# Sixteen-head cross-attentions: four row groups of TensorE share the score matmuls, and each context's column scores go four heads at a time

## The chip, the cores and the metric

One core of one Trainium2 chip runs the whole program. The metric is the device time of one execution in microseconds (us), as the median of several runs. The kernel before takes 1945.53 us (median of 3 runs, 1936.75 to 1956.92).

## The reference, cut to what matters

A model of four layers; each has a cross-attention block and a feed-forward block, on x of 4 sequences x 512 tokens x 128 features, with a context of 4 x 77 x 64. The change touches three of the attentions: layer 0's (`l0x`, 16 heads of 8 features), the second one of layer 1 (`a2`, 16 heads of 32 features) and layer 3's (`l3x`, 16 heads of 8). All three are the same computation:

```python
qh = (q @ Wq + bq).reshape(B, LQ, HEADS, D_K).transpose(0, 2, 1, 3)      # 512 queries, 16 heads
kh = (k @ Wk + bk).reshape(B, LKV, HEADS, D_K).transpose(0, 2, 1, 3)     # 77 keys
vh = (v @ Wv + bv).reshape(B, LKV, HEADS, D_K).transpose(0, 2, 1, 3)
scores = jnp.einsum('bhqd,bhkd->bhqk', qh, kh) * scale
attn = jax.nn.softmax(scores, axis=-1)
out = jnp.einsum('bhqk,bhkd->bhqd', attn, vh)
...
return concat @ Wo + bo
```

Everything else (the layer norms, layer 1's causal attentions, the routed experts of layers 1 to 3) is computed too and is not changed.

## The kernel before, in words

Features lie on the 128 partitions, tokens along the free dimension. The sequences are worked on two at a time (`U = range(SLOTS)`, u = 0 and 1); a hardware loop makes two turns (`Fori(0, TURNS)`), and each turn runs `l0x`, `a2` and `l3x` once. So there are six passes through `cross(tag, dh)`: four with dh = 8 and two with dh = 32. Each engine has its own `cross` (TensorE from line 618, ScalarE from 1562, VectorE from 1920); they meet at counted semaphores only. The order of the work on each engine is written out by hand.

A pass does this:

- **Row scores R(u, a)**, a = 0 to 7, `rowscores` (matmuls on lines 641 for dh = 8 and 645 for dh = 32): queries on the partitions, for two values of c, four heads' 77 keys each. With dh = 8 a matmul uses one row group (c = 2 hf + b, hf = a % 2); with dh = 32 it uses all 128 rows, so nothing can run beside it. VectorE takes their maxima (`maxima`, line 1927).
- **cut off and turned**: the maxima are split in two bf16 halves (`cut_off`) and transposed (`turned`, line 654), and ScalarE copies them out (`shifted`, line 1565).
- **Column scores T(u, a)**, a = 0 to 7, `colscores` (line 670): keys on the partitions, 512 queries, for two heads (k = a // 2, c = 2 hf + b). Two float32 matmuls of 32 x 512, then two bf16 ones that subtract the maxima in the same PSUM bank. I call these last **less**, after the variable. ScalarE takes the exponentials of both heads (`exp`, line 1574).
- **sums** (line 681, dh = 32 alone) and **values** (line 695): four matmuls side by side in four column groups over all 77 keys, for the four heads of one k. They use all the rows.

The two sequences overlap: R(0, .) come first, alone. In what I call **phase 1** TensorE does T(0, a), R(1, a) for a = 0 to 7, with values(0, k) behind a = 3, 5, 7 and once more at the end, and then turned(1). In **phase 2** it does T(1, a), with values(1, k) behind a = 3, 5, 7. A **pair** below is the stretch of two values of a, with the sums and values that belong to it.

R and T share three slots of two PSUM banks each, in turn: `cplace` gives the place of each step in that ring, `cbefore` tells what was three places before, and `free(x)` makes TensorE wait until VectorE's maximum or ScalarE's exponential has read it. In phase 1 T(0, a) has place 9 + 2a and R(1, a) place 10 + 2a. So R(1, a) waits for the exponential of T(0, a - 1), and T(0, a) for the maximum of R(1, a - 2). In phase 2 T(1, a) waits for the exponential of T(1, a - 3). `values(u, k)` waits for the exponential of T(u, 2k + 1) with dh = 8; with dh = 32 it waits for ScalarE's copy `o` (line 1586) of the values before, which ScalarE does behind two later exponentials.

## Time and profile before

| | |
|---|---|
| median of 3 runs | 1945.53 us (1936.75 to 1956.92) |
| profiled execution, whole | 1932.59 us |
| its span, first to last instruction | 1930.5 us |
| mean granted TensorE clock in it | 0.87 of full |
| instructions | 22528 |

### The profile page before, as it was taken

What the parts mean: (1) busy time and instruction counts of PE and PEld (TensorE: products, weight loads), DVE (VectorE), ACT (ScalarE), POOL (GpSimd) and SP (SyncE); (2) the same over time, 40 slices, a digit from 0 to 9 for tenths busy, and PEclk for the clock granted to TensorE, in tenths of its full rate; (3) what the DMA queues carried; (4) which work ended last, traced back from release to release, by engine and by line L of the source; (5) the groups of instructions that cost most, each with busy time, mean ns of one, the idle gap of its engine ahead of it and who ended that gap; (6) DMA issues with size and microseconds to landing.
All of it is one profiled execution on the core that took longest, in us unless ns stands there. A gap on an engine that the chain in (4) does not pass through costs nothing.

```text
span 1930.5 us, 22528 instructions
## 1 busy us (share of the span) xinstructions
PE 1643.6 (85%) x9068; PEld 762.3 (39%) x9068; DVE 880.0 (46%) x1746; ACT 715.9 (37%) x1267; POOL 146.9 (8%) x207
## 2 busy tenths in 40 slices
PE   5748999989899989997648999989899989988487
PEld 2323333332344536633323323332343436543274
DVE  4474664253456353324474663353456352337312
ACT  2333455324435225232332455323445125243133
POOL 0000011100012000000000111100012000002232
PEclk9768899989989699956768999989999689889688
DMA  4000000000000100000000000000000100002241
GB/s 178 1 1 0 1 2 1 1 1 1 0 1 1 44 1 1 1 1 2 1 1 0 1 1 1 0 1 1 0 1 2 44 1 1 1 33 44 62 135 59
DMA packets 18107, 30.17 MB, mean 16 GB/s; under 512 B 4640, under 2 KB 12640, under 8 KB 17104
## 3 DMA queue, kind: packets, MB, share of 16 engines
q1 hardware_dynamic: 16752, 26.10, 4.2%
q0 software_dynamic: 1248, 2.59, 0.4%
q8 instruction: 74, 1.21, 0.3%
q14 instruction: 33, 0.27, 0.0%
HBM read 23.49 MB, written 5.19 MB: 15 GB/s over the span
## 4 chain that ended last, share of the span: by engine, by line
PE 78%; DVE 12%; ACT 7%; issue 2%; DMA 1%; SPq 0%; POOL 0%; POOLq 0%; DVEq 0%; ACTq 0%
PE ps L783 8%; PE ps L881 5%; PE ps L670 5%; PE ps L613 3%; PE ps L815 3%; PE ps L1323 3%; PE ps L1335 3%; PE ps L1020 3%; PE ps L695 3%; PE ps L1012 3%; PE ps L932 2%; PE ps L829 2%; PE ps L1242 2%; PE ps L912 2%; PE ps L804 2%
## 5 line engine op out<-in xcount | busy, mean ns | idle before, releaser
L2000 DVE TENSOR_REDUCE peak<-ps 128x1 f32<-128x512 f32 x256 | 165.4, 686 | 119.0 <-PE ps L783 118.4
L1620 ACT ACTIVATE big<-ps 128x512 f32<-128x512 f32 x256 | 139.6, 595 | 133.8 <-PE ps L806 126.9
L783 PE MATMUL ps<-pp,qT 32*128 32x512 f32 x512 | 169.5, 714 | 3.5 <-DVE peak L2000 2.1
L804 PE MATMUL ps<-qT,pp 32*128 32x512 f32 x512 | 160.4, 649 | 0.0
L1641 ACT ACTIVATE big<-ps 128x512 f32<-128x512 f32 (+3 forms) x256 | 100.3, 436 | 112.5 <-PE ps L912 111.7
L2037 DVE TENSOR_REDUCE crest<-ps 128x2 f32<-128x512 f32 (+3 forms) x128 | 105.2, 825 | 65.7 <-PE ps L887 65.6
L1574 ACT ACTIVATE big<-ps 77x1024 f32<-77x1024 f32 x96 | 94.7, 1019 | 95.8 <-PE ps L670 95.2
L912 PE MATMUL ps<-qT,pp 32*128 32x256 f32 (+3 forms) x512 | 124.4, 494 | 0.9 <-ACT big L1641 0.9
L1927 DVE TENSOR_REDUCE small<-ps 128x8 f32<-128x616 f32 x96 | 74.2, 797 | 102.8 <-PE ps L641 58.1
L881 PE MATMUL ps<-pp,qT 32*128 32x384 f32 (+3 forms) x512 | 109.2, 501 | 9.5 <-DVE crest L2037 8.5
L1555 ACT ACTIVATE sq<-ps 128x512 f32<-128x512 f32 x52 | 31.1, 597 | 204.4 <-PE ps L613 204.4
L670 PE MATMUL ps<-qT,kt 32*77 32x512 f32 x384 | 94.1, 741 | 9.8 <-ACT spare L1565 9.6
L783 PEld LDWEIGHTS ps<-pp,qT 32*128 32x128 f32 x512 | 59.2, 202 | 83.4 <-DVE peak L2000 65.9
L542 POOL TENSOR_SCALAR_AFFINE_SELECT big<-big 128x512 f32<-128x512 f32 x64 | 40.8, 637 | 616.4 <-PE ps L815 616.4
L560 POOL TENSOR_SCALAR_AFFINE_SELECT big<-big 128x512 f32<-128x512 f32 x64 | 40.8, 637 | 555.9 <-ACT big L1641 555.9
L1879 DVE TENSOR_TENSOR xn<-ps,rs 128x512 f32<-128x512 f32 x40 | 27.7, 692 | 94.0 <-ACT rs L1560 94.0
L815 PE MATMUL ps<-big,cst 128*32 128x512 f32 x512 | 68.1, 604 | 0.0
L1012 PE MATMUL ps<-xn,w_l 128*128 128x512 f32 x96 | 51.7, 699 | 18.1 <-DVE xn L1884 18.1
L1778 ACT ACTIVATE big<-ps,w_l 128x512 f32<-128x512 f32 x64 | 44.0, 687 | 59.1 <-PE ps L1323 57.5
L695 PE MATMUL ps<-big,vx 77*32 77x512 f32 x384 | 58.3, 690 | 6.0 <-ACT qT L1586 6.0
L1335 PEld LDWEIGHTS ps<-pt,big 128*128 128x128 f32 x512 | 59.4, 192 | 6.7 <-issue 6.7
L806 PE MATMUL ps<-spare,minus 32*128 32x512 bf16 x256 | 61.4, 377 | 0.0
(484 smaller groups left out, 2775.3 us busy)
## 6 DMA issues: line engine op xcount, KB each, us to landing
big<-in_w SPq DMA_DIRECT2D x23, 256.0 KB
pt<-in_l2w SPq DMA_DIRECT2D x2, 2048.0 KB, 7.5
w_l<-in_l SPq DMA_DIRECT2D x1, 3086.0 KB, 17.3
pp<-in_w SPq DMA_DIRECT2D x1, 2048.0 KB, 9.6
big<-by_expert SPq DMA_DIRECT2D x23, 66.0 KB, 2.0
by_expert<-cst SPq DMA_DIRECT2D x1, 1472.0 KB, 16.3
cst<-in_const SPq DMA_DIRECT2D x1, 1298.0 KB, 5.8
w_l<-in_l SPq DMA_DIRECT2D x1, 1218.0 KB, 8.0
```

The source lines that it names most:

```text
L670: mm = pe.matmul(PSB[cbank(x) + b][0:KC, :], keys, query, start=not less, stop=less, tile_position=(32 * c, 0))
L695: mm = pe.matmul(PSB[k // 2 if dh == 8 else 0][32 * c:32 * c + 32, :], vx[:, u, at:at + 32], cprob(u, k)[:, c, :], start=dh == 32 or k % 2 ...
L783: pe.matmul(rbank(x), qT[at, u, k, 128 * i:128 * i + 128], keyT(u, k)[at, :], start=True, stop=True, tile_position=(32 * c, 0)).then_inc(* ...
L804: pe.matmul(tbank(y), keyT(u, k)[at, 128 * j:128 * j + 128], qT[at, u, k, :], start=True, stop=False, tile_position=(32 * c, 0))
L815: mm = pe.matmul(PSB[1][32 * c:32 * c + 32, :], K["col8"][:, 128 * k + 32 * c:128 * k + 32 * c + 32], prob(n)[:, c, :], start=n % 16 == 0, ...
L881: pe.matmul(PSB[pbank(x) + c % 2][:, 0:hi], qT[at, u, k, 128 * i:128 * i + 128], keyT(u, k)[at, 0:hi], start=True, stop=False, tile_positi ...
L912: pe.matmul(tbank(y)[:, lo:512], keyT(u, k)[at, 128 * j:128 * j + 128], qT[at, u, k, lo:512], start=True, stop=True, tile_position=(32 * c ...
L1012: pe.matmul(scb(c), w[:, 128 * c:128 * c + 128], src(u), start=True, stop=True)\
L1335: mm = pe.matmul(lin(u)[:, 128 * i:128 * i + 128], hid[u][:, c, 128 * i:128 * i + 128], W2[:, 128 * c:128 * c + 128], start=c == 0, stop=c ...
L1620: A(prob(m)[:, TURN_OF[g], :], tbank(tplace(m, g)), ACT.Exp).then_inc(*SCALAR.did("a1", "exp", m, g))
L2000: v.tensor_reduce(peak[:, p // 4 % 2, i, c:c + 1], rbank(ring(p, c)), AX.X, ALU.max)\
L2037: v.tensor_reduce(crest[:, u, i, 2 * h:2 * h + 2, k], ps[:, b:b + 2, 0:hi], AX.X, ALU.max)\
```

## The change

In the order of the diff:

- The ring's places change. With dh = 8 phase 1 keeps the places (T(0, a) at 9 + 2a, R(1, a) at 10 + 2a). With dh = 32 they go in fours: T(2k), T(2k + 1), R(2k), R(2k + 1). So T(0, 2k) waits for the exponential of T(0, 2k - 1), and R(1, 2k + 1) for that of T(0, 2k).
- With dh = 8 the half of the row groups that R(1, a) uses is turned round (`half_of`): it takes the two that T(0, a) leaves.
- `colscores(u, a)` becomes single steps `colscore(u, a, b, less)`. `colscores4(u, k)` issues the float32 matmuls of four heads and then their four less; it replaces two `colscores` in all of phase 2, and in phase 1 with dh = 32. The new `colscores(a)`, for phase 1 with dh = 8, issues R(1, a) ahead of T(0, a)'s less where a is odd, and behind it where a is even.
- In phase 1 with dh = 8 values(0, k - 1) moves from behind R(1, 2k + 1) to between R(1, 2k) and T(0, 2k + 1). With dh = 32 sums and values stand behind each group of T, T, R, R, as before in count. The last values(0, 3) stays ahead of turned(1).
- The number of matmuls, their shapes, the reductions, the exponentials and the copies stay as they are.

```diff
--- before.py
+++ after.py
@@ -301,16 +301,18 @@
 
         TURN_OF = (2, 3, 0, 1)
 
-        def cplace(kind, u, a=0):
-
-
-            if kind == "R":
-                return a if u == 0 else 10 + 2 * a
+        def cplace(dh, kind, u, a=0):
+
+
+
             if kind == "turned":
                 return 8 if u == 0 else 25
-            return 9 + 2 * a if u == 0 else 26 + a
-
-        def cbefore(x):
+            if (kind == "R") == (u == 0):
+                return a if u == 0 else 26 + a
+            later = kind == "R"
+            return 9 + 2 * a + later if dh == 8 else 9 + 4 * (a // 2) + a % 2 + 2 * later
+
+        def cbefore(dh, x):
 
             z = x - 3
             if z < 0:
@@ -319,9 +321,16 @@
                 return "R", 0, z
             if z == 8 or z == 25:
                 return "turned", z // 25, 0
-            if z < 25:
-                return ("T", 0, (z - 9) // 2) if z % 2 else ("R", 1, (z - 10) // 2)
-            return "T", 1, z - 26
+            if z > 25:
+                return "T", 1, z - 26
+            z -= 9
+            if dh == 8:
+                return ("R", 1, z // 2) if z % 2 else ("T", 0, z // 2)
+            return ("R", 1, 2 * (z // 4) + z % 2) if z % 4 >= 2 else ("T", 0, 2 * (z // 4) + z % 2)
+
+        def half_of(dh, u, a):
+
+            return (a + u) % 2 if dh == 8 else a % 2
 
         def cbank(x):
             return 2 + 2 * (x % 3)
@@ -619,7 +628,7 @@
 
 
                 def free(x):
-                    h = cbefore(x)
+                    h = cbefore(dh, x)
                     if h and h[0] == "R":
                         pe.wait_ge(*VECTOR[tag, "max", h[1], h[2]])
                     elif h and h[0] == "turned":
@@ -628,8 +637,8 @@
                         pe.wait_ge(*SCALAR[tag, "exp", h[1], h[2]])
 
                 def rowscores(u, a):
-                    i, hf = a // 2, a % 2
-                    x = cplace("R", u, a)
+                    i, hf = a // 2, half_of(dh, u, a)
+                    x = cplace(dh, "R", u, a)
                     free(x)
                     if a == 0:
                         pe.wait_ge(*VECTOR[tag, "kv", u])
@@ -647,7 +656,7 @@
                     mm.then_inc(*TENSOR.did(tag, "R", u, a))
 
                 def turned(u):
-                    x = cplace("turned", u)
+                    x = cplace(dh, "turned", u)
                     pe.wait_ge(*VECTOR[tag, "cut", u])
                     free(x)
                     for i in range(4):
@@ -655,21 +664,38 @@
                                           cut[:, i].rearrange("p c r -> p (c r)"), identb[:])
                     mm.then_inc(*TENSOR.did(tag, "turned", u))
 
-                def colscores(u, a):
-                    k, hf = a // 2, a % 2
-                    x = cplace("T", u, a)
-                    free(x)
-                    if a == 0:
-                        pe.wait_ge(*SCALAR[tag, "shift", u])
+                def colscore(u, a, b, less):
+                    k, c = a // 2, 2 * (a % 2) + b
+                    x = cplace(dh, "T", u, a)
+                    if not less and b == 0:
+                        free(x)
+                        if a == 0:
+                            pe.wait_ge(*SCALAR[tag, "shift", u])
+                    at = slice(32 * c, 32 * c + 32)
+                    keys = minus[at, k:k + 1].to_broadcast([32, KC]) if less else kt[at, u, k, :]
+                    query = shift[at, u, :] if less else qT[at, u, 0 if dh == 8 else k, :]
+                    mm = pe.matmul(PSB[cbank(x) + b][0:KC, :], keys, query, start=not less, stop=less,
+                                   tile_position=(32 * c, 0))
+                    if less and b:
+                        mm.then_inc(*TENSOR.did(tag, "T", u, a))
+
+                def colscores4(u, k):
+
                     for less in (False, True):
-                        for b in (0, 1):
-                            c = 2 * hf + b
-                            at = slice(32 * c, 32 * c + 32)
-                            keys = minus[at, k:k + 1].to_broadcast([32, KC]) if less else kt[at, u, k, :]
-                            query = shift[at, u, :] if less else qT[at, u, 0 if dh == 8 else k, :]
-                            mm = pe.matmul(PSB[cbank(x) + b][0:KC, :], keys, query, start=not less, stop=less,
-                                           tile_position=(32 * c, 0))
-                    mm.then_inc(*TENSOR.did(tag, "T", u, a))
+                        for a in (2 * k, 2 * k + 1):
+                            for b in (0, 1):
+                                colscore(u, a, b, less)
+
+                def colscores(a):
+
+                    colscore(0, a, 0, False)
+                    colscore(0, a, 1, False)
+                    if a % 2:
+                        rowscores(1, a)
+                    colscore(0, a, 0, True)
+                    colscore(0, a, 1, True)
+                    if a % 2 == 0:
+                        rowscores(1, a)
 
                 def sums(u, k):
                     if dh == 8:
@@ -725,20 +751,27 @@
                 for a in range(8):
                     rowscores(0, a)
                 turned(0)
-                for a in range(8):
-                    colscores(0, a)
-                    rowscores(1, a)
-                    if a >= 3 and a % 2:
-                        sums(0, (a - 3) // 2)
-                        values(0, (a - 3) // 2)
+                for k in range(4):
+                    if dh == 8:
+                        colscores(2 * k)
+                        if k:
+                            values(0, k - 1)
+                        colscores(2 * k + 1)
+                    else:
+                        colscores4(0, k)
+                        rowscores(1, 2 * k)
+                        rowscores(1, 2 * k + 1)
+                        if k:
+                            sums(0, k - 1)
+                            values(0, k - 1)
                 sums(0, 3)
                 values(0, 3)
                 turned(1)
-                for a in range(8):
-                    colscores(1, a)
-                    if a >= 3 and a % 2:
-                        sums(1, (a - 3) // 2)
-                        values(1, (a - 3) // 2)
+                for k in range(4):
+                    colscores4(1, k)
+                    if k:
+                        sums(1, k - 1)
+                        values(1, k - 1)
                 if dh == 8:
                     heads(0, 0)
                     heads(0, 1)
@@ -1562,12 +1595,12 @@
             def cross(tag, dh):
                 def shifted(u):
                     act.wait_ge(*TENSOR[tag, "turned", u])
-                    A(shift[:, u, :], PSB[cbank(cplace("turned", u))].bitcast(BF16)[:, 0:512], ACT.Identity)\
+                    A(shift[:, u, :], PSB[cbank(cplace(dh, "turned", u))].bitcast(BF16)[:, 0:512], ACT.Identity)\
                         .then_inc(*SCALAR.did(tag, "shift", u))
 
                 def exp(u, a):
                     k, hf = a // 2, a % 2
-                    b = cbank(cplace("T", u, a))
+                    b = cbank(cplace(dh, "T", u, a))
                     act.wait_ge(*TENSOR[tag, "T", u, a])
                     if u and hf == 0:
                         act.wait_ge(*TENSOR[tag, "AV", 0, k])
@@ -1919,8 +1952,8 @@
 
             def cross(tag, dh, bv=None):
                 def maxima(u, a):
-                    i, hf = a // 2, a % 2
-                    b = cbank(cplace("R", u, a))
+                    i, hf = a // 2, half_of(dh, u, a)
+                    b = cbank(cplace(dh, "R", u, a))
                     v.wait_ge(*TENSOR[tag, "R", u, a])
                     top = tops(u)[:, i, 2 * hf:2 * hf + 2, :] if dh == 8 else \
                         tops(u)[:, i, :, 2 * hf:2 * hf + 2].rearrange("p c k -> p k c")
```

## Rows read from the trace of the kernel before

**Rows 1.** the page: span, busy time by engine, the chain by engine

```profile
span 1930.5 us, 22528 instructions
...
PE 1643.6 (85%) x9068; PEld 762.3 (39%) x9068; DVE 880.0 (46%) x1746; ACT 715.9 (37%) x1267; POOL 146.9 (8%) x207
...
PE 78%; DVE 12%; ACT 7%; issue 2%; DMA 1%; SPq 0%; POOL 0%; POOLq 0%; DVEq 0%; ACTq 0%
```

**Rows 2.** windows, phase 1: length, busy of PE PEld DVE ACT POOL, clock

```profile
1687.65:1705.27 17.62, 16.05 (x112) 5.88 (x113) 7.23 (x11) 8.32 (x9) 0.00 (x0) 0.91 0.00 1
428.51:455.58 27.07, 27.07 (x144) 9.78 (x145) 6.85 (x10) 9.73 (x11) 0.00 (x0) 1.00 0.00 1
```

**Rows 3.** windows of the four whole passes of l0x and l3x

```profile
41.97:72.84 30.87, 28.66 (x205) 11.63 (x205) 7.98 (x12) 17.61 (x20) 0.00 (x0) 0.89 0.00 1
824.21:867.09 42.88, 41.73 (x205) 14.56 (x205) 7.98 (x12) 17.93 (x20) 0.00 (x0) 0.57 0.00 1
905.43:939.18 33.75, 31.91 (x204) 12.44 (x204) 7.98 (x12) 17.67 (x20) 0.00 (x0) 0.79 0.00 1
1687.65:1717.66 30.01, 27.57 (x204) 10.74 (x204) 7.98 (x12) 17.50 (x20) 0.00 (x0) 0.95 0.00 1
```

**Rows 4.** the chain of waits, 440 to 448 us (a2): start, us, what

```profile
440.30 1.23 PE ps L670 x6
441.53 1.23 PE ps L645 x4
...
445.23 1.00 PE ps L681 x8
446.23 0.86 PE ps L695 x8
```

**Rows 5.** the chain of waits, 51 to 56 us (l0x)

```profile
51.33 1.25 PE ps L670 x8
...
52.60 1.03 ACT big L1574
...
53.68 0.79 PE ps L641 x4
54.46 1.00 PE ps L695 x8
```

**Rows 6.** timeline of l0x, 51 to 53 us: start, us, engine, line, records

```profile
51.26 1.16 PE L670 MATMUL ps<-qT,kt 32*77 32x512 f32 x6
...
52.18 0.38 PE L670 MATMUL ps<-spare,minus 32*77 32x512 bf16 x2
...
52.26 0.59 PE L670 MATMUL ps<-qT,kt 32*77 32x512 f32 x2
...
52.40 0.68 PE L641 MATMUL ps<-kt,qT 32*128 32x308 f32 x4
```

**Rows 7.** timeline of l0x, end of phase 1 and a stretch of phase 2

```profile
58.58 1.92 PE L695 MATMUL ps<-big,vx 77*32 77x512 f32 x16
...
60.44 0.40 PE L654 MATMUL ps<-identb,spare 128*128 128x128 bf16 x4
...
66.32 1.16 PE L670 MATMUL ps<-qT,kt 32*77 32x512 f32 x8
```

**Rows 8.** the chain of waits, 462 to 472 us (a2, phase 2)

```profile
466.32 1.06 PE ps L695 x8
467.38 1.25 PE ps L670 x12
...
468.65 1.93 ACT big L1574 x2
470.58 0.49 ACT qT L1586
```

**Rows 9.** windows of TensorE alone around a fall of its clock (l0x)

```profile
39.00:42.00 3.00, 0.43 (x6) 1.00 0.00 0
42.00:45.00 3.00, 3.00 (x16) 0.55 0.00 0
```

## The prediction

> **What bounds the kernel now.** The page first: TensorE is busy for 85% of the span and holds 78% of the chain that ended last [rows 1]. That share says nothing about one stage, so the next view is the windows: phase 1 of a pass takes 27.07 us in `a2` at full clock with PE busy for all of it, and 17.62 us in the best of the four dh = 8 passes, at a granted clock of 0.91 [rows 2]. The four whole dh = 8 passes take 30.87, 42.88, 33.75 and 30.01 us, in the order of their clocks, 0.89, 0.57, 0.79 and 0.95 [rows 3]: the same instructions, so a low clock costs more here than most edits could give.
>
> The chain of waits of `a2` shows a pair in phase 1 as pure TensorE work: T 1.23, R 1.23, twice each, then sums 1.00 and values 0.86 [rows 4], 4 x 1.23 + 1.86 = 6.78 us. Four times 4.92 and four times 1.86 make 27.1, which is the window's 27.07 [rows 2]. Nothing but TensorE's order of work bounds it.
>
> The chain of `l0x` shows something else: T 1.25, an exponential 1.03, R 0.79, values 1.00 and the small gaps 0.02 and 0.05 between them [rows 5], 4.14 us a pair. It goes round a loop: T(even), its exponential, R(odd) that wants the banks so freed, values, T(even) again. The second T and the first R of the pair aren't in it. The timeline tells why: six float32 records of T begin in the 1.16 us from 51.26, four of which are one step, and the first less comes only at 52.18, R at 52.40 [rows 6]. So T(odd) started ahead of the less and the R that stand before it in the program, in the two row groups that these leave free. In phase 2 eight float32 records, four heads, fit in 1.16 us [rows 7]. Four row groups are at work side by side already.
>
> **Phase 1 of a2** (two passes). Removed: one T stretch in each pair, since four heads' T go together. A T of four heads costs 1.25 us on the chain (12 records, [rows 8]), as much as one of two heads. R(2k) follows, 1.23. R(2k + 1) waits for the exponential of T(2k): 1.25 + 0.02 + 1.03 + 0.05 = 2.35 us after the group began, while TensorE is done with T and R(2k) at 1.25 + 1.23 = 2.48 at most. Then R(2k + 1) 1.23, sums and values 1.86: 5.4 to 5.6 us in place of 6.78, so 1.2 to 1.35 saved; I take 1.3. What is late next is that exponential, level with TensorE. The other new wait, T(2k + 2) for the exponential of T(2k + 1), is over at 1.27 + 2 x 1.03 = 3.3, before the group's own R ends. Four pairs, two passes: 8 x 1.3 = **10.4 us saved**. The bounds are 8 x 1.2 = 9.6 and 8 x 1.35 = 10.8.
>
> **Phase 2, all six passes.** T of four heads instead of two and two. Nothing to take: at both kinds of pass the eight f32 records are already side by side [rows 7, 8]. In `a2` the pair is values 1.06, T 1.25, two exponentials 1.93, the copy `o` 0.49 [rows 8], a loop that ScalarE closes, and no wait in it moves. The less of T(2k) now stands behind T(2k + 1)'s wait for the exponential of T(2k - 2); the timeline has both T's in one group with no hole in it [rows 7], so that wait is met or nearly so. Zero, with 0.1 us a pair either way, 24 pairs, for the range: 2.4 us.
>
> **Phase 1 with dh = 8** (four passes). The ring keeps its places, so R(1, a) waits for the exponential of T(0, a - 1) as before. Values sit behind R(even) now, so the loop is: exponential of T(odd) 1.03, R(even) 0.79, values 1.00, T(odd) 1.25, gaps 0.07. That is 4.14 again. R(odd) moves beside T(odd), but neither it nor the even T was in the loop. The loop gives nothing back; the ends change. Counted from T(0, 0): T 1.25, gap 0.02, exponential 1.03, gap 0.05, so R(1, 1) starts at 2.35, and T(0, 1)'s less stand behind it and its wait. They take 0.38 [rows 6] and a little to get through, so the second exponential starts near 2.8 and R(1, 2) near 3.9; values(0, 0) near 4.7, values(0, 2) two loops on, near 13.0. Then 1.00 + 1.25 + 0.02 + 1.03 + 0.05 = 3.35 to values(0, 3), which has to wait for T(0, 7) and its exponential, at 16.3, and about 0.9 until turned(1): 17.2 us at full clock. Before, values(0, 2) and values(0, 3) go back to back and turned(1) starts 1.86 after the first of them (58.58 and 60.44, [rows 7]). The pass at clock 0.91 spent 2 x 0.09 x 17.62 = 3.2 us at half speed, which cost it at most 1.6 us: 16.0 to 17.6 at full clock, my estimate 16.2. So each pass **loses about 1.1 us**, 4.4 in all; less if half speed cost that pass nothing. Upper bound: the longer tail with nothing won at the start, 3.35 + 0.9 - 1.86 = 2.4 a pass, 9.6. Lower bound, below nothing: R's 0.79 leaves the loop in four pairs, -3.2 a pass, -12.6. I take 1.1, since all the pieces of the loop have rows and none of them is taken out. VectorE and ScalarE do the same instructions; R(1, 7)'s maximum and the cut off are ready before values(0, 3) in this account.
>
> **Sum.** -10.4 + 0 + 4.4 = -6.0 us. The profiled execution took 1932.59 us, so it would take 1926.6. It lies 12.9 below the median of the runs shown, and I move the sum to that: 1945.5 - 6.0 = **1939.5 us**.
>
> **A rule against a row.** The rows have T(odd) start before the less of T(even) [rows 6]. The Trainium skill, "TensorE: Matmul & The Clock Gate", section "Part 3: Packing small matmuls", says otherwise: matmuls start and end in program order, and only weight loads are pulled ahead. By that rule half the array stands idle in every T of two heads, and the change is worth what rival C gives. This trace disagrees, with 51.26 to 52.42 for the six records against 52.18 for the less.
>
> **Rivals.**
> - **A, the forecast**, 1939.5: `a2` gains, the dh = 8 ends lose. Chance 0.60.
> - **B, TensorE bounds dh = 8 too.** With R(odd) beside T(odd) the loop sheds R's 0.79 in each pair: -12.6, and with `a2` -23.0, 1922.5. For it: PE is busy 16.05 of 17.62 us [rows 2]. Against it: busy time counts four groups as one, and R(even) still waits for an exponential. 0.13.
> - **C, strict order.** Were T's of two heads one after another now, each pair of phase 1 with dh = 8 (16) and of phase 2 (24) would shed one float32 stretch of 1.16 [rows 7]: 40 x 1.16 = 46 us more, 1889. The trace contradicts it: eight records fit in 1.16. 0.02.
> - **D, the clock** (slower than before). TensorE was at full clock and did 0.43 us of work in 3, and the next 3 us were granted 0.55 [rows 9]. The new order has TensorE wait for two exponentials in a row at the start of a dh = 8 pass and once more ahead of values(0, 3). If that held the three faster passes at the clock of the slowest, they would cost 12.0 + 9.1 + 12.9 = 34 us [rows 3]: 1973.5. It decides from one such pass on, since 9 to 13 us outweigh the 6 saved. Against it: in `a2`'s phase 2 TensorE waits through 1.93 + 0.49 us of ScalarE in every pair [rows 8], longer than any new wait. 0.13.
> - **E, the clock the other way.** The slowest pass gets the clock of the best: -12.9, 1926.6. Nothing in the change calls for it but the shift in time. 0.12.
>
> **How the numbers follow.** About 1% (19 us) is what a measurement of this kernel can tell from no change; the three runs before lie 20 us apart. Faster by over 1% (under 1926.1): C, most of B, half of E and a tail of A, 0.20. Slower by over 1% (over 1965.0): most of D and a tail of A, 0.11. Within: 0.69. The range takes A with its bounds: all the gains, 10.8 + 12.6 + 2.4 = 25.8 us, give 1919.7, all the losses, 9.6 + 2.4 - 9.6 = 2.4, give 1947.9. Above that comes half the spread of the runs, 10 us, and the smaller cases of D: **1920 to 1964**.
>
> **What would show it.** Right: `a2`'s phase 1 lasts about 21.7 to 22.3 us at full clock, T with 12 records on the chain, two R's behind it. Phase 2 of `a2` keeps 4.8 us a pair. Dh = 8: 4.1 us between values, the last T(0, 7), its exponential and values(0, 3) one after another at the end of phase 1, which lasts 17 us or more at full clock. Wrong: values in phase 1 with dh = 8 come at 3.4 us (B); R(1, even) starts before the exponential that frees its banks; `a2` keeps 6.8 us (four heads' T don't go together beside their less); or the granted clock of the four passes falls together (D).

## The result and the profile after

| | before | changed |
|---|---|---|
| median | 1948.28 us (1922.76 to 1978.95, 8 runs) | 1957.61 us (1954.88 to 1964.05, 8 runs) |
| profiled execution's span | 1930.5 us | 1952.8 us |
| mean granted TensorE clock in it | 0.870 | 0.851 |

The ratio is 1.0118, 95% interval 1.0079 to 1.0157, but it leaves out runs more than 1.5% above the fastest of their kernel, which here are the longer runs of the kernel before alone. By the medians of all runs the changed kernel is 9.3 us slower, 0.5%. By the means of all its 15 runs and of 101 runs of the kernel before (1956.8 and 1950.0 us) it is 6.8 +- 1.9 us slower. So it is slower by 0.3 to 0.5%, where a gain of 6 us was forecast. The spread of the runs is the subject here, so medians and means below are over all runs.

The page of the changed kernel, its span, busy times and chain, with the same instructions as before and 19 us more of busy PE:

```profile
span 1952.8 us, 22528 instructions
...
PE 1662.9 (85%) x9068; PEld 762.7 (39%) x9068; DVE 879.3 (45%) x1746; ACT 715.8 (37%) x1267; POOL 146.6 (8%) x207
...
PE 78%; DVE 12%; ACT 6%; issue 2%; DMA 1%; POOL 1%; SPq 0%; POOLq 0%; DVEq 0%; ACTq 0%
```

Phase 1 of three dh = 8 passes and of one `a2` pass, in windows (start and end; length; busy time and records of PE, PEld, DVE, ACT, POOL; granted clock; DMA), to be held against [rows 2]. The dh = 8 pass that is left out, the second, takes 22.06 us at 0.72:

```profile
41.77:63.82 22.05, 20.10 (x112) 6.87 (x113) 7.32 (x11) 8.54 (x9) 0.00 (x0) 0.71 0.00 1
910.73:938.84 28.11, 26.70 (x113) 8.28 (x113) 7.32 (x11) 8.65 (x9) 0.00 (x0) 0.50 0.00 1
1699.66:1727.77 28.11, 26.70 (x112) 8.28 (x113) 7.32 (x11) 8.65 (x9) 0.00 (x0) 0.50 0.00 1
433.84:455.77 21.93, 21.93 (x145) 8.55 (x145) 6.85 (x10) 9.29 (x11) 0.00 (x0) 1.00 0.00 1
```

The whole dh = 8 passes, from the start of phase 1 to that of the last values as in [rows 3]:

```profile
41.77:80.32 38.55, 35.75 (x205) 12.36 (x205) 8.07 (x12) 17.83 (x20) 0.00 (x0) 0.70 0.00 1
833.69:872.22 38.53, 35.69 (x204) 12.38 (x204) 8.07 (x12) 17.83 (x20) 0.00 (x0) 0.70 0.00 1
910.73:956.31 45.58, 43.33 (x204) 13.65 (x204) 8.07 (x12) 17.94 (x20) 0.00 (x0) 0.55 0.00 1
1699.66:1741.96 42.30, 40.05 (x205) 13.59 (x205) 8.07 (x12) 17.93 (x20) 0.00 (x0) 0.60 0.00 1
```

`a2` gave what was forecast: 21.93 us for 27.07, and its second pass is the same length. Two dh = 8 passes have a granted clock of 0.50 from end to end of phase 1, 28.11 us each, where the last one had 0.91 and 17.62 before. The four whole passes take 164.96 us together, where they took 137.51 [rows 3]: 27.5 us more. Phase 1 of `a2` takes 10.3 us less in its two passes, and the column scores of `a2` behind it 1.9 us more (13.79 and 13.74 us at 0.92 and 0.93 for 12.84 and 12.83 at 1.00). That makes some 19 of the 22.3 us by which the two spans differ. Of the 27.5, some 7 us are the order's own cost at full clock, as measured below; the rest, about 20 us, is the clock.

The chain of waits of `a2`, against [rows 4]. T of four heads, two R's with no hole, sums, values, 5.51 us for 6.78:

```profile
443.05 1.25 PE ps L677 x12
444.30 2.40 PE ps L654 x8
446.70 1.00 PE ps L707 x8
447.69 0.86 PE ps L721 x8
```

The chain of `l0x` from 54 us, at full clock, against [rows 5]: R(even), values, T(odd) with R(odd) beside it, an exponential, round again in 4.13 us; at the end values from 59.49, the last exponential from 61.75 and values(0, 3) only at 62.82:

```profile
54.57 0.79 PE ps L650 x4
55.36 1.00 PE ps L721 x8
56.36 0.47 PE ps L677
56.82 0.27 PE ps L650 x3
57.09 0.52 PE ps L677 x6
...
57.63 1.03 ACT big L1607
...
59.49 1.00 PE ps L721 x8
...
61.75 1.03 ACT big L1607
...
62.82 1.06 PE ps L721 x8
```

The start of phase 1 in the last `l3x` pass, in the timeline, at half clock. R(1, 0) runs beside T(0, 0), from 1699.78. T(0, 1)'s float32 records run next, and then R(1, 1) and T(0, 1)'s less come only at 1703.18 and 1703.20, when the exponential of T(0, 0) is over. TensorE is idle for 0.30 us ahead of them:

```profile
1699.66 1.14 PE L677 MATMUL ps<-qT,kt 32*77 32x512 f32 x2 [0.78 <-ACT spare L1598]
...
1699.78 1.40 PE L650 MATMUL ps<-kt,qT 32*128 32x308 f32 x4
...
1700.56 1.48 PE L677 MATMUL ps<-qT,kt 32*77 32x512 f32 x4
...
1701.41 0.66 PE L677 MATMUL ps<-spare,minus 32*77 32x512 bf16 x2
...
1702.11 1.02 ACT L1607 ACTIVATE big<-ps 77x1024 f32<-77x1024 f32 x1 [2.60 <-PE ps L677]
...
1703.18 0.88 PE L650 MATMUL ps<-kt,qT 32*128 32x308 f32 x2 [0.30 <-ACT big L1607]
...
1703.20 0.64 PE L677 MATMUL ps<-spare,minus 32*77 32x512 bf16 x2
```

### The profile page after: what moved, and what is told of

The parts are those of the page before. It is cut to its first block, busy times and chain, and to the rows that moved or that the text cites. A ratio compares the mean times of both kernels' runs of the same rounds, so it can differ in the third digit from the quotient of the medians.

```text
span 1952.8 us, 22528 instructions
## 1 busy us (share of the span) xinstructions
PE 1662.9 (85%) x9068; PEld 762.7 (39%) x9068; DVE 879.3 (45%) x1746; ACT 715.8 (37%) x1267; POOL 146.6 (8%) x207
## 4 chain that ended last, share of the span: by engine, by line
PE 78%; DVE 12%; ACT 6%; issue 2%; DMA 1%; POOL 1%; SPq 0%; POOLq 0%; DVEq 0%; ACTq 0%
PE ps L816 7%; PE ps L677 5%; PE ps L914 5%; PE ps L622 3%; PE ps L848 3%; PE ps L721 3%; PE ps L1356 3%; PE ps L1368 3%; PE ps L1053 3%; PE ps L1045 3%; PE ps L965 2%; PE ps L1275 2%; PE ps L862 2%; PE ps L837 2%; PE ps L945 2%
## 5 line engine op out<-in xcount | busy, mean ns | idle before, releaser
L677 PE MATMUL ps<-qT,kt 32*77 32x512 f32 x384 | 103.2, 864 | 10.1 <-ACT spare L1598 9.6
L721 PE MATMUL ps<-big,vx 77*32 77x512 f32 x384 | 64.0, 745 | 9.5 <-ACT qT L1619 5.1
L650 PE MATMUL ps<-kt,qT 32*128 32x308 f32 x256 | 60.8, 604 | 3.9 <-ACT big L1607 2.2
```

The source lines that it names most:

```text
L677: mm = pe.matmul(PSB[cbank(x) + b][0:KC, :], keys, query, start=not less, stop=less, tile_position=(32 * c, 0))
L721: mm = pe.matmul(PSB[k // 2 if dh == 8 else 0][32 * c:32 * c + 32, :], vx[:, u, at:at + 32], cprob(u, k)[:, c, :], start=dh == 32 or k % 2 ...
```

## The experiments

**How runs are compared.** Every run lists its time and mean granted clock, so its time at half clock is 2 x (1 - clock) x time. Over the 101 runs of the kernel before that went with the experiments (mean 540 us at half clock), time = 1731.4 us + 0.405 x (us at half clock), with a residual of 2.1 us (one standard deviation): nearly all of their spread, 1916 to 1992 us, is this one quantity. "At equal clock" below is a kernel's mean distance from that line, with its standard error. It tells roughly what the instructions cost apart from the clock; the time at half clock tells the rest. It is a fit, not a measurement of each stage, and where a stage pays less than 0.405 us for a us at half clock, its own cost comes out too low.

| kernel | runs | median us | ratio to before (95%) | mean of all runs, less its group's before | us at half clock (its group's before) | at equal clock |
|---|---|---|---|---|---|---|
| before, with the experiments | 101 | 1947.3 | | | 540 | 0 |
| changed | 8 | 1957.6 | 1.0118 (1.0079 to 1.0157) | +8.2 +- 6.1 | 585 | -10.0 +- 0.8 |
| changed, again | 7 | 1955.7 | 1.0096 (1.0062 to 1.0130) | +9.3 +- 3.2 | 580 (530) | -11.0 +- 1.0 |
| a2 alone | 12 | 1943.5 | 0.9968 (0.9914 to 1.0022) | -15.6 +- 6.2 | 543 (554) | -10.8 +- 0.6 |
| dh = 8 alone | 6 | 1982.8 | 1.0131 (1.0057 to 1.0206) | +29.1 +- 8.3 | 622 (554) | +2.1 +- 1.4 |
| phase 2 alone | 10 | 1961.8 | 1.0022 (0.9951 to 1.0092) | +6.4 +- 6.3 | 567 (554) | +1.5 +- 0.6 |
| a2 and phase 2 | 12 | 1945.0 | 0.9999 (0.9953 to 1.0045) | -2.6 +- 4.9 | 566 (543) | -12.5 +- 0.6 |
| late values | 12 | 1942.6 | 1.0053 (1.0005 to 1.0101) | -1.0 +- 4.2 | 561 (530) | -13.6 +- 0.6 |
| less first | 12 | 1946.0 | 1.0042 (1.0008 to 1.0077) | -0.7 +- 3.4 | 554 (530) | -10.5 +- 0.9 |
| halves only | 12 | 1932.1 | 0.9948 (0.9905 to 0.9991) | -14.2 +- 4.3 | 525 (530) | -12.2 +- 0.4 |
| wait in a2 | 4 | 1995.7 | 1.0276 (1.0190 to 1.0361) | +35.8 +- 13.3 | 619 (554) | +9.8 +- 0.4 |
| halves, extra matmuls | 6 | 1914.1 | 0.9854 (0.9807 to 0.9902) | -35.6 +- 3.2 | 463 (543) | -4.0 +- 0.4 |
| halves, wait instead | 12 | 1945.7 | 1.0069 (1.0017 to 1.0121) | -2.9 +- 5.8 | 555 (534) | -10.3 +- 0.5 |
| changed, extra matmuls | 14 | 1942.5 | 0.9946 (0.9899 to 0.9992) | -6.0 +- 6.0 | 535 (543) | -3.5 +- 0.9 |
| before, extra matmuls | 12 | 1925.5 | 0.9915 (0.9870 to 0.9960) | -21.2 +- 4.5 | 473 (543) | +6.3 +- 0.5 |
| a2 alone, extra matmuls | 6 | 1911.7 | 0.9851 (0.9774 to 0.9928) | -36.4 +- 6.3 | 460 (534) | -5.6 +- 0.5 |

The runs were made in four groups, and the kernel before had medians of 1956.9 (beside a2 alone, dh = 8 alone, phase 2 alone, wait in a2), 1943.6 (changed again, late values, less first, halves only), 1947.3 (halves, changed and before with extra matmuls, a2 and phase 2) and 1947.4 (halves with a wait, a2 alone with extra matmuls). Each ratio is to its own group's. A value behind +- is one standard error; each window below is from one execution, and where that was the longest or the shortest of its kernel's runs, the text says so.

### The parts of the change, each alone

In the a2 kernel the dh = 8 passes and phase 2 are as before. `colscores2(u, a)` is what the kernel before calls `colscores(u, a)`. The edit that is left, beside the ring's places in fours for dh = 32:

```diff
-                        for a in (2 * k, 2 * k + 1):
-                            colscores2(0, a)
-                            rowscores(1, a)
+                        colscores4(0, k)
+                        rowscores(1, 2 * k)
+                        rowscores(1, 2 * k + 1)
```

> The change in phase 1 of a2 alone (four heads' T, then R, R); dh = 8 and phase 2 as before. Theory 1 (the new order of the dh = 8 passes lowers the clock): phase 1 of a2 is 21.9 us in place of 27.07, twice, the clock of the rest is that of before, and the kernel is 10 us faster, near 1938 at a median before of 1948. Theory 2 (any shift in time of the work against the clock's own times changes the granted clock): phase 1 of a2 is the same 21.9, but the clock of other stages that are not edited moves, by up to 20 us of time either way.

Measured: 10.8 us under the line at equal clock, phase 1 21.93 us in one `a2` pass. The mean of all runs is 15.6 +- 6.2 us lower than the kernel before of the same group. Windows of an `l3x` pass and of the other `a2` pass, from the shortest of its 12 runs:

```profile
821.45:839.08 17.63, 16.05 (x113) 5.90 (x113) 7.22 (x11) 8.31 (x9) 0.00 (x0) 0.91 0.00 1
1268.52:1291.94 23.42, 23.42 (x145) 9.17 (x145) 6.84 (x10) 9.28 (x11) 0.00 (x0) 0.93 0.00 1
```

The `l3x` pass is at 17.63 us and 0.91, the pattern of [rows 2]; the second `a2` pass has a clock of 0.93 and takes 23.42. The part is a gain, at equal clock of the size forecast.

The dh = 8 kernel has the new phase 1 in the four dh = 8 passes alone, with the turned halves:

```diff
-                        for a in (2 * k, 2 * k + 1):
-                            colscores2(0, a)
-                            rowscores(1, a)
-                        if k:
-                            values(0, k - 1)
+                        colscores(2 * k)
+                        if k:
+                            values(0, k - 1)
+                        colscores(2 * k + 1)
```

> The change in phase 1 of the four dh = 8 passes alone; a2 and phase 2 as before. Theory 1: slower by 15 to 35 us, with two or more of the four passes at half clock all through and phase 1 at 22 to 28 us. Theory 2: slower by the 4 to 8 us that the later values(0, 3) costs, give or take a clock that moves in stages that are not edited.

Measured: 1982.8 us, 26 us over the kernel before of the same group, and 68 us more at half clock; at equal clock 2 us. Windows of phase 1 of an `l0x` pass and of the unedited `a2`, from the longest of its 6 runs:

```profile
43.18:71.30 28.12, 26.71 (x113) 8.29 (x113) 7.32 (x11) 8.64 (x9) 0.00 (x0) 0.50 0.00 1
1336.49:1378.15 41.66, 41.66 (x144) 14.01 (x145) 6.85 (x10) 9.72 (x11) 0.00 (x0) 0.63 0.00 0
```

All four dh = 8 passes look like the first line. Theory 1 holds for them. But the second line is a stage that nobody edited, at 0.63 and 41.67 us, so theory 2 isn't wrong either: the clock moves elsewhere too.

Phase 2 alone:

```diff
-                    colscores2(1, 2 * k)
-                    colscores2(1, 2 * k + 1)
+                    colscores4(1, k)
```

> Column scores four heads at a time in phase 2 alone, all passes. Both theories: no change in the order in which the float32 records run, under 2 us; theory 2 allows a moved clock all the same.

Measured: 1.5 us at equal clock and a ratio that holds 1. Its windows show phase 1 of an `l3x` and of an `a2` pass, both with the order of before:

```profile
831.55:857.82 26.27, 25.96 (x112) 8.73 (x113) 7.23 (x11) 8.65 (x9) 0.00 (x0) 0.50 0.00 1
1294.52:1336.19 41.67, 41.67 (x144) 13.95 (x145) 6.85 (x10) 9.73 (x11) 0.00 (x0) 0.63 0.00 0
```

The same instructions as in [rows 2], at 26.27 and 41.67 us. So the old order has the half clock too, in some executions, and its `a2` phase 1 is not always the 27.07 that I took from one profile.

One combination of the parts more: phase 1 of `a2` and all of phase 2 new, with phase 1 of dh = 8 as before. Its edit is that of the a2 kernel and that of phase 2 together:

> The changed kernel with phase 1 of dh = 8 as before. 10 to 12 us under the kernel before at equal time at half clock; in the median within 4 us of the kernel with only the turned halves.

Measured: -12.5 at equal clock, as expected, but a median of 1945.0, 13 us over the halves-only kernel of another group. The clock made the difference (566 us at half clock against 525); I had expected the two level. In part the groups differ: against their own the two kernels have +23 +- 13 and -5 +- 11 us at half clock.

### What a wait does to the clock

Twenty more copies in VectorE's cut off, in both `a2` passes of the kernel before:

```diff
+                    for _ in range(20 if dh == 32 and u == 0 else 0):
+                        chain(v.tensor_copy(cut[:, :, :, 0:8:2], tops(u)))
```

> The kernel before with twenty more copies of 0.24 us in VectorE's cut off of a2 for the first sequence, some 5 us in each of the two a2 passes in which TensorE waits; nothing else. They cost 10 us by themselves. Theory 1: 10 us slower, the dh = 8 passes at the clocks of before. Theory 2: stages behind a2 change their clock, and the time is off 10 us by as much as the runs before differ, 10 to 20 us.

Measured: 10 us by the line, as they cost themselves, and 619 us at half clock: 39 us over the kernel before in the median. Only four runs, so the size is rough. In the shortest of them TensorE was busy for 9.14 of the 16.11 us of row scores with the wait in them, the clock fell there, and the phase 1 behind it, which nobody edited, took 34.42 us at 0.78. Against the 27.07 of [rows 2] that is 7 us more for a wait of 5; but the same stage was at 36.8 and 41.67 us in a kernel without the wait, so one profile doesn't prove it. The theories aren't told apart by this run.

### What in the dh = 8 order costs the clock

The changed kernel was run again, beside three kernels that undo parts of its dh = 8 order. The new phase 1 of `a2` and the new phase 2 stay in all of them.

> The changed kernel once more, as the one to compare the next three with on the same chip. All theories: some 10 us under the kernel before at an equal time spent at half clock, and more time at half clock than before (585 us against 554 in the runs so far), so near or above it in the median.

Measured: as expected, 580 us at half clock, three of four dh = 8 phases 1 at 28.11 us.

Late values: values(0, k - 1) back behind R(1, 2k + 1).

```diff
                         colscores(2 * k)
-                        if k:
-                            values(0, k - 1)
                         colscores(2 * k + 1)
+                        if k:
+                            values(0, k - 1)
```

> The changed kernel with values(0, k - 1) of the dh = 8 passes back behind R(1, 2k + 1); R(1, odd) stays ahead of T(0, odd)'s less. Theory 3 (the place of values, and the wait ahead of values(0, 3) that it leaves, costs the clock): phase 1 of the dh = 8 passes is back at 17 to 21 us in most, time at half clock back at 540 to 555 us, 10 to 15 us faster than the changed kernel. Theory 4 (less behind R's wait at the start costs the clock): as the changed kernel, 28.1 us in most passes, within 4 us of it.

Less first: less stays ahead of R(1, a) for every a.

```diff
-                    if a % 2:
-                        rowscores(1, a)
                     colscore(0, a, 0, True)
                     colscore(0, a, 1, True)
-                    if a % 2 == 0:
-                        rowscores(1, a)
+                    rowscores(1, a)
```

> The changed kernel with less ahead of R(1, a) for odd a too; values stay between R(1, 2k) and T(0, 2k + 1). Theory 3: as the changed kernel. Theory 4: phase 1 at 17 to 21 us in most passes and 10 to 15 us faster than the changed kernel.

Halves only: both edits together.

> The changed kernel with both undone, so that of the dh = 8 phase 1 only the turned halves of R(1, a) are left. Theories 3 and 4 both: 10 to 15 us faster than the changed kernel. If the turned halves themselves cost the clock (theory 5), it is no faster.

Measured: the time at half clock goes from 580 to 561 +- 8, 554 +- 4 and 525 +- 8 us, so the undone parts give back 19 and 26 us of it and both together 55. By these means theories 3 and 4 each hold in part, and theory 5 falls. What the theories said of single passes did not come: phase 1 was not back at 17 to 21 us in most passes of late values or less first. The medians are 13, 10 and 24 us under the changed kernel's. Halves only beats both kernels: 0.9948 of before, 0.9905 to 0.9991; it has the gain of `a2` in it. Windows of phase 1 of less first, of late values (the longest of its 12 runs) and of halves only:

```profile
898.79:926.47 27.68, 26.57 (x112) 8.29 (x113) 7.32 (x11) 8.65 (x9) 0.00 (x0) 0.50 0.00 1
```

```profile
833.29:859.91 26.62, 25.45 (x112) 8.35 (x112) 7.32 (x11) 8.65 (x9) 0.00 (x0) 0.50 0.00 1
```

```profile
821.66:848.23 26.57, 26.53 (x113) 8.86 (x113) 7.22 (x11) 8.64 (x9) 0.00 (x0) 0.50 0.00 1
```

At half clock throughout, phase 1 is 28.11 us with both, 27.68 with less first, 26.62 with late values, 26.57 with neither, and 26.27 as before. That is the order's own cost, and the smaller part. How many of the four passes have that clock can't be ranked from one or two profiles a kernel: four with dh = 8 alone, two and three in the two profiles of the changed kernel, three each with late values and with less first, two with halves only.

**The same fall, another return.** The traces settle more, since they have the moments at which the granted clock fell and came back. In 28 of the 32 dh = 8 passes with the order before or the changed one (and no extra matmuls), it had fallen before phase 1 began, in the row scores R(0, .), which no edit of the order touches. So passes with the same moment of the fall can be compared; moments are us from the start of phase 1, before it with a minus:

| order of phase 1, dh = 8 | fell at | back at | passes |
|---|---|---|---|
| as before | -3.56 to -3.45 | 3.26 to 3.38 | 6 |
| changed | -3.49 to -3.48 | 34.06 to 34.07 | 5 |
| less first | -3.44 | 3.39 | 1 |
| late values | -3.45 | 13.61, down again 17.0 to 30.7 | 1 |
| halves only | -3.38, -3.34 | 3.45, 3.48 | 2 |
| as before | -2.48 | 7.76 | 1 |
| late values | -2.49 | 31.65 | 1 |
| changed | -2.74, -2.70 | 45.05, 45.09 | 2 |
| as before | -3.09 to -2.97 | 3.73 to 14.10 | 3 |
| changed | -3.04 to -3.03 | 41.33 to 41.34 | 2 |
| as before | -3.69 to -3.66 | 37.27 to 37.30 | 4 |
| as before | -4.46, -4.44 | 43.32, 43.35 | 2 |
| changed | -4.50 to -4.43 | 12.57 to 12.64, down again 22.8 to 33.1 | 3 |
| less first, late values, halves only | -4.50 to -4.23 | 33.06 to 39.94 | 7 |

The first 4 us of phase 1 and the 13 us behind them, TensorE alone, of the kernel with `a2` and phase 2 new (order as before), then the changed kernel, then less first, then late values:

```profile
833.71:837.71 4.00, 3.92 (x20) 0.58 0.00 0
837.71:850.71 13.00, 11.50 (x92) 1.00 0.01 1
1699.66:1703.66 4.00, 3.70 (x18) 0.50 0.00 0
1703.66:1716.66 13.00, 13.00 (x60) 0.50 0.00 1
829.47:833.47 4.00, 4.00 (x20) 0.58 0.00 0
833.47:846.47 13.00, 10.97 (x88) 1.00 0.01 1
914.17:918.17 4.00, 3.70 (x18) 0.50 0.00 0
918.17:931.17 13.00, 12.24 (x66) 0.63 0.01 1
```

So from the same entry the changed order stays at half clock until 34 us after the start, well into phase 2, where the order before is back at full clock after 3.3. With R(1, 1) ahead of T(0, 1)'s less TensorE does 3.70 us of work in the first 4, with less first 4.00, and only the latter has the clock back at once: that part of theory 4 is seen here, in one pass. The late values alone bring the return from 34 to 13.6 us, before another fall. The table has two limits. A fall 0.1 to 0.2 us earlier costs the order before as much (37.3 us), and after a fall at -4.5 the changed order does better. So the order decides the return, but together with the moment of the fall.

The changed order also loses a full clock: each of its 3 passes that ended phase 1 at full clock (and the one with extra matmuls below) fell again within 1.4 us behind it, and none of the 14 with the order before did. Which of the two parts does that isn't shown: the one pass of less first kept its clock, the one of late values lost it at 17.0 us.

**The new order of `a2` does the opposite.** Where the clock fell 1.0 to 1.1 us into phase 1 of `a2`, the old order had it back at 31.7 to 31.8 us (3 passes) and the new one at 4.4 to 4.5 (8 passes). TensorE alone, from 4.5 us into phase 1 on, old order (dh = 8 alone) and new (a2 alone, extra matmuls):

```profile
1340.99:1366.49 25.50, 25.50 (x65) 0.50 0.00 0
```

```profile
1276.92:1293.42 16.50, 16.50 (x107) 1.00 0.00 1
```

Over all profiles the old phase 1 of `a2` takes 27.07 to 41.67 us (10 passes, mean 35.1) and the new one 21.93 to 23.45 (22 passes, mean 22.6). So where the clock falls near its start the new order of `a2` gains more than its 10 us at equal clock; the 15.6 +- 6.2 us of a2 alone leave room for that but don't show it.

### Work in the wait

Two matmuls on a bank that nobody reads, where TensorE waits for VectorE ahead of turned(0) in the dh = 8 passes ([rows 9] has that wait):

```diff
                 for a in range(8):
                     rowscores(0, a)
+                if dh == 8:
+                    for _ in range(2):
+                        pe.matmul(PSB[0][:, :], ident, qT[:, 0, 0, :], start=True, stop=True)
                 turned(0)
```

> The kernel with only the turned halves, plus two float32 matmuls of 128 x 512 with 128 rows on a bank that nobody reads, in the two us in which TensorE waits for VectorE ahead of turned(0) in the four dh = 8 passes. If the idle time there is what brings half clock to phase 1: phase 1 at full clock in most passes, 40 us or more less at half clock, and 12 to 25 us faster than without them. If not: no change within 4 us, since they fit in the wait.

> The changed kernel with the same two matmuls. If the clock alone makes it slower than before: phase 1 of dh = 8 drops from 28.1 to about 18.5 us where the clock stays full, and it is 10 us or more under the kernel before. If its own waits at the start keep the clock down: 28.1 us as now.

> The kernel before with the same two matmuls: as much as they give the clock of the others, 10 to 25 us faster, or no change.

Measured: all three at less time at half clock than the same kernel without them (463 for 525, 535 for 585 and 580, 473 for 540 us). They don't fit in the wait wholly: the row scores take 9.87 to 10.83 us in place of 8.31 to 8.71, which is most of the 5 to 8 us that they cost at equal clock. With that in it, halves with extra matmuls takes 1914.1 us, 33 us under before. By the means of all runs against each group's before, the matmuls give some 21 us in the kernel before, in halves only and (below) in a2 alone, and 15 +- 7 us in the changed kernel. Of the two outcomes named ahead for the latter, the second came in three passes of four: 28.1 us as without them. Windows of the changed kernel with them: row scores and phase 1 of the second `l0x` pass, then of the last `l3x` pass:

```profile
912.84:922.71 9.87, 8.71 (x41) 3.75 (x41) 6.91 (x11) 0.60 (x1) 0.00 (x0) 0.83 0.00 0
922.71:940.45 17.74, 14.82 (x113) 5.08 (x113) 7.32 (x11) 8.42 (x9) 0.00 (x0) 1.00 0.00 1
1695.36:1706.19 10.83, 9.67 (x41) 4.12 (x41) 6.97 (x11) 0.60 (x1) 0.00 (x0) 0.69 0.00 0
1706.19:1734.31 28.12, 26.71 (x113) 8.28 (x113) 7.32 (x11) 8.64 (x9) 0.00 (x0) 0.50 0.00 1
```

Phase 1 of the kernel before with them, and of halves only with them; the latter's row scores are 10.83 us at 0.69 too:

```profile
828.20:844.22 16.02, 14.19 (x113) 5.55 (x113) 7.23 (x11) 8.32 (x9) 0.00 (x0) 1.00 0.01 1
```

```profile
1674.61:1692.02 17.41, 16.29 (x113) 6.18 (x113) 7.22 (x11) 8.42 (x9) 0.00 (x0) 0.90 0.00 1
```

Two things are to be seen. At full clock from end to end phase 1 is 17.74 us in the new order and 16.02 in the old one: 1.7 us of order. And where the row scores enter at 10.83 us and 0.69, with the clock already fallen, the halves-only kernel gets it back early in phase 1 (17.41 us, 0.90) and the changed one keeps 0.50 to the end, 28.12 us. Three of its four passes did that. The extra matmuls don't keep the clock from falling. The row scores have 0.83 with them in the better passes; there the clock is back at 1.1 to 1.8 us ahead of phase 1.

The same 1.4 us of delay without the work:

```diff
+                    for _ in range(6 if dh == 8 and u == 0 else 0):
+                        chain(v.tensor_copy(cut[:, :, :, 0:8:2], tops(u)))
```

> The kernel with only the turned halves, with six more copies of 0.24 us in VectorE's cut off ahead of turned(0) in the four dh = 8 passes: the same 1.4 us later start of phase 1 that the two extra matmuls made, but with TensorE idle in it. If the matmuls helped by their work: no pass wholly at full clock, as much time at half clock as with the turned halves only (525 us) or more, 1935 us or above. If they helped by the shift in time: as with the matmuls, 460 us at half clock and 1915 us.

```profile
34.32:44.29 9.97, 5.53 (x38) 2.57 (x37) 8.14 (x17) 0.60 (x1) 0.00 (x0) 0.79 0.00 0
44.29:70.86 26.57, 26.53 (x112) 8.91 (x113) 7.22 (x11) 8.65 (x9) 0.00 (x0) 0.50 0.00 1
```

These windows are from the longest of its 12 runs. The shift is the same, 9.97 us of row scores, with PE busy for 5.53 in place of 8.71. The time at half clock is 555 us, 30 +- 9 more than without the delay and 92 +- 6 more than with the matmuls, and the median 1945.7. It was the work, not the shift.

The fastest combination:

> The change in phase 1 of a2 alone, with the two extra matmuls ahead of turned(0) in the dh = 8 passes; all else as before. If what each gave adds up: phase 1 of dh = 8 16.0 us at full clock, that of a2 21.9, 1912 us, the fastest of all; with the clock falling more often than with the turned halves, up to 1925.

Measured: 1911.7 us, 0.9851 of before (0.9774 to 0.9928), 36 us under it. It can't be told from halves with extra matmuls (1914.1). Phase 1 of its last `l3x` pass, which enters as the changed kernel's did (row scores of 10.83 us at 0.70) and gets the clock back:

```profile
1672.52:1690.15 17.63, 16.12 (x113) 5.92 (x113) 7.23 (x11) 8.33 (x9) 0.00 (x0) 0.90 0.00 1
```

## Why the prediction was wrong, point by point

- **The clock was taken as it stood in one profile.** This is the step that failed. The sum set the clock at nothing and left it to rival D with a chance of 0.13. The changed kernel spends 585 us at half clock where the one before spends 540; by the fit that is 45 x 0.405 = 18 us, against the 10.0 under the line at equal clock, +8 in all, and the medians lie 9.3 apart. Stage by stage, the dh = 8 passes went from clocks of 0.89, 0.57, 0.79 and 0.95 to 0.70, 0.70, 0.55 and 0.60 and took 27.5 us more where 4.4 were forecast and D had said 34; "the granted clock of the four passes falls together" was the prediction's own sign of being wrong. The first of D's two places is borne out by the passes that can be compared, the start, where R(1, 1) and the less behind it wait for an exponential. The second, the wait ahead of values(0, 3), is in part argued: late values gave back 19 +- 8 us at half clock.
- **The time lies in the range, by luck.** 1957.6 is between 1920 and 1964, but the range reached that high for the spread of the runs and the smaller cases of D, not for a loss in four passes of this size.
- **The argument against D was wrong.** I held that `a2`'s phase 2 waits longer at full clock. That shows what a stretch bears that is at full clock. The dh = 8 passes mostly begin after a stretch with little work, at or behind a fall of the clock [rows 9], and there the question is whether the order gets the clock back. In the profiles without extra matmuls, 9 of 12 new-order phases 1 stay at 0.50 to the end (dh = 8 alone and the changed kernel twice) and 6 of 20 old-order ones (before, a2 alone, phase 2 alone, wait in a2, a2 and phase 2); their means are 26.6 and 21.1 us, 22 us over four passes. Phase 2, right behind, has a clock below full in 12 of the 12 and in 6 of the 20. The Trainium skill, "TensorE: Matmul & The Clock Gate", "Loop structure matters more than you think", says that "Whether your matmuls stay warm is determined by your loop nest"; these runs agree, for an order within one pass.
- **a2**: forecast 10.4 us, measured 2 x (27.07 - 21.93) = 10.3 in the two profiles and 10.8 +- 0.6 at equal clock. Both the T group of 1.25 and the level finish of exponential and R were as said. Right; that the old order took 34.4 to 41.7 us in 7 of the 8 passes of other profiles was not in the one profile that the sum went by.
- **Phase 2**: forecast zero, measured 1.5 +- 0.6 us slower at equal clock alone, and 1.7 +- 0.9 faster where it was added to `a2`. Within its bound and not told from zero.
- **The loop of dh = 8**: forecast 4.14 us, measured 4.13. B, its contrary, is out. **The ends**: forecast 1.1 us a pass (17.2 - 16.2 is 1.0), measured 1.7 at full clock (17.74 - 16.02, in the kernels with extra matmuls) and 1.84 at half (28.11 - 26.27), so 7 us for four passes in place of 4.4. The fit shows only 2.1 +- 1.4 for dh = 8 alone; it takes time at half clock as equally dear everywhere (0.405), and in these phases 1 it is 0.37 to 0.39, so I trust the windows. The rest of the difference is not explained.
- **E, the clock the other way**: out, 0.851 for 0.870 in the whole kernel. **C, strict order**: out (its 1889 counts the gain of `a2` alone; with the whole sum it would be 1893). In the changed kernel R(1, 0) stands behind T(0, 0)'s less and starts at 1699.78, the less at 1701.41. What the Trainium skill says ("TensorE: Matmul & The Clock Gate", "Part 3: Packing small matmuls"), that matmuls start in program order, does not hold for different row groups here.
- **The sum without the clock** was -6.0. The windows at one clock give -10.3 + 6.9 = -3.4 and the fit -10.0 +- 0.8; the forecast lies between them. The signs of the instruction terms were right; the sign of the result was not.

What stays open: the clock of stages that nobody edited also differs between executions (the old `a2` phase 1 at 27.07, 36.8 and 41.67 us). The moment at which it falls differs by some tenths of a us and decides much of it, but why one execution has one moment and another not isn't shown.

## What to carry to other kernels

Where the granted clock isn't 1.00 all through, regress the runs' times on their time at half clock before believing a profile: here it told a change of 10 us from a spread of 75. A new order is to be judged by what it does right behind a fall of the clock, not only by its loop: an order that made TensorE wait for an exponential in its first 4 us stayed at half clock for 34 us, where another was back at full clock after 3.3. Compare passes in which the clock fell at the same moment. And two otherwise useless matmuls in a wait bought more, some 21 us in three kernels, than any part of the rearranging (15.6 +- 6.2 us in `a2`, a loss in the dh = 8 passes).

## What the runs showed of the hardware

- Matmuls in other row groups overtake earlier ones: in the kernel before T(0, odd) starts ahead of T(0, even)'s less [rows 6], in the changed one R ahead of a less by 1.6 us. Two T's of two heads run side by side however they are issued, which is why issuing them together gave nothing in phase 2.
- TensorE can stay at half clock while it works without a gap: in the old phase 1 of `a2` it was busy for 25.50 of 25.50 us at 0.50, with matmuls of 32 x 512 and 128 x 308 float32 in turn. The same work ran at full clock in other passes (27.07 us of 27.07).
- Idle time costs more than itself: 1.4 us a pass of waiting raised the time at half clock by 30 us, and the same time with matmuls in it lowered it by 62, against the same kernel with neither.
- The changed kernel's times lie closer together (1952 to 1964 us in 15 runs) than those of the one before (1916 to 1992 in 101); the eight dh = 8 phases 1 in its two profiles have one of two lengths, 22.06 or 28.11 us, to 0.01.
